# Macaron stack on one core: when the relative-distance rows of the first attention are read back from DRAM

## The chip, the cores and the metric

The kernel runs on one core of one Trainium2 chip (trn2). The metric is the device time of one execution in microseconds (us); where several executions were timed, the median is given.

## What is computed

The reference is a stack of four "macaron" layers in float32 over a stream x of 16 sequences of 256 tokens with 128 features. Each layer adds half a feed-forward block, an attention, and half a feed-forward block again, each on a layer-normalised copy of x. The four kinds are: product-key experts with an attention with relative distances (layer 0); windowed attention and a gated feed-forward block with a rotary attention (layer 1); routed experts with full attention (layer 2); an int8 gated block with a latent attention (layer 3).

Only the attention of layer 0 matters here. It has 16 heads of 8 features, and its scores are a product of queries and keys plus a term for the distance between two tokens, which is computed against all distances and then shifted row by row:

```python
def _rel_shift(x):
    B, H, Lq, Lr = x.shape
    xp = jnp.concatenate([jnp.zeros((B, H, Lq, 1), x.dtype), x], axis=-1)
    xp = xp.reshape(B, H, Lr + 1, Lq)
    return xp[:, :, 1:].reshape(B, H, Lq, Lr)[..., Lr - Lq:]
x = x + _L0_attn_ref(_layernorm(x, axis=-1), L0_attn_Wq, L0_attn_Wk, L0_attn_Wv, L0_attn_Wr, L0_attn_u_bias, L0_attn_v_bias)
```

## The kernel before, in words

The stream X stays in SBUF, transposed (features on partitions, 4096 tokens along the free side). The blocks run one after another, each in a `Phase` with its own tiles and semaphores, with a barrier at the end. Within a phase the program of every engine is written out by hand, and the engines meet at semaphores.

`strip_attention(..., "rel", ...)`, whose tiles are named `l0att_...`, is the attention of layer 0. A **pair** is two heads of one sequence: there are 8 pairs in a sequence and 128 in all. A **half** t (0 or 1) is 128 of the 256 queries. Every engine walks through steps j, and does parts of several pairs in each; step j stands at place g = j % 8 of its sequence. The steps of all engines are made by `steps`: the steps before the loop written out, then a loop (`Fori`) of 7 passes with 16 steps each, then the last steps written out.

The distances of pair j+3 are prepared in step j, three steps ahead of the scores that need them:

- TensorE, `distance_rows` (L613): both heads' distance terms of one half into the PSUM tile `XP`, of which there is one.
- ScalarE, `keep_rows` (L772): `XP` copied into `XS`, 128 partitions by 768 floats. `XS` has room for two pairs, two halves each, so the copy for pair j waits until the write of pair j-2, same half, has landed (`written`). It counts up `x_kept`.
- SyncE, `write` (L513): waits for `x_kept` and stores that half of `XS`, 384 KB, to the DRAM tensor `shifted_rows`, which holds eight pairs.
- SyncE, `read` (L521): waits until that write has landed (`written`) and until VectorE has done with the pair four before (`shifted`), and then loads the half again with rows that are two elements shorter than they were stored, 256 KB, into `BD`. This shifts row r by r places, as `_rel_shift` does. `BD` holds four pairs.
- VectorE, `shift` (L861): waits for the two halves (`landed`), adds `BD` to the scores in `SC` and takes the row's extreme, four times for a pair (two heads, two halves). Both halves of `BD` are needed for the first head.

In its own step j VectorE does `shift` of pair j, head 0, both halves; the copy of the transposed exponentials of pair j-1 (L869); some work once in a sequence; `shift` of head 1; the strips (L874); and a second copy L869. ScalarE's step is: `XS` half 0 of pair j+3, two exponentials of pair j (L793), the strips of pair j+5 (L783), `XS` half 1, two more exponentials. TensorE's step is: distance rows half 0 (L613), strips (L649), transposes (L637), distance rows half 1, every second step the values (L673), the third strip (L655), transposes, the scores of pair j+1 (L626), and `extras` at places 2, 3, 4, 6 and 7 of the sequence.

SyncE has one instruction stream. What it waits for in a `read` also holds back the `write` behind it:

```python
def step(b, j):
    write(b, j + 3, 0)
    read(b, j + 2, 1)
    write(b, j + 3, 1)
    read(b, j + 3, 0)
```

`held` is the wait of both, and adds a count to a semaphore that nobody waits for (`passed`).

Of the kernel before, what the change touches and what calls it, by code (L numbers as in the profile page):

```python
# [132 lines left out]
def load(eng, dst, src, sem):  # L133

    return eng.dma_start(dst, src, allow_slow_non_contiguous=True).then_inc(sem, 16)
# [273 lines left out]
def strip_attention(nc, tag, kind, R, XN, A, W, ident, shifted=None):  # L409
# [19 lines left out]
    with Phase(nc, tag) as ph:  # L429
# [38 lines left out]
        def until(eng, sem, value):  # L468

            if not isinstance(value, int) or value > 0:  # L470
                eng.wait_ge(sem, value)

        def exists(b, j):
            return not isinstance(b, int) or 0 <= 16 * b + j < PAIRS
# [4 lines left out]
        def steps(eng, step):  # L479
            for j in range(-6, BEGIN):  # L480
                step(0, j)
            with eng.Fori(0, NB // 2 - 1) as b:
                for j in range(BEGIN, BEGIN + 16):
                    step(b, j)
            for j in range(BEGIN, 16 + TAIL):
                step(NB // 2 - 1, j)

        with nc.Block() as block:
            @block.sync
            def _(sp):  # L490
                load(sp, wq[:, :], W["q"], sm["loaded"])
                load(sp, wk[:, :], W["k"], sm["loaded"])
                load(sp, wv[:, :], W["v"], sm["loaded"])
                if not rel:
                    load(sp, wqx[:, :], W["q_crossed"], sm["loaded"])
                    load(sp, wkx[:, :], W["k_crossed"], sm["loaded"])
                    load(sp, wo[:, :], W["o"], sm["loaded"])
                    load(sp, mask[:, :, :], A["causal"], sm["loaded"])
                    load(sp, rt[:, :, :], A["rope8"], sm["loaded"])
                    return  # L500
                load(sp, ub[:, :], W["u"], sm["loaded"])
                load(sp, vb[:, :], W["v_bias"], sm["loaded"])
                load(sp, wr[:, :], W["r"], sm["loaded"])
                load(sp, emb[:, :], A["rel_emb"], sm["loaded"])

                def held(sem, value):
                    until(sp, sem, value)
                    sp.sem_inc(sm["passed"], 1)

                def write(b, j, t):  # L510
                    if exists(b, j):
                        held(sm["x_kept"], 2 * (16 * b + j) + t + 1)
                        sp.dma_start(shifted[j % 8, t], XS[:, j % 2, t, :, :]).then_inc(written[j % 2][t], 16)  # L513

                def read(b, j, t):

                    if exists(b, j):
                        held(written[j % 2][t], 16 * (8 * b + j // 2 + 1))
                        held(sm["shifted"], 4 * (16 * b + j - 3))
                        rows = shifted[j % 8, t].rearrange("r c -> (r c)")[2 * P - 2:2 * P - 2 + 2 * P * (WIN - 1)]  # L520
                        sp.dma_start(BD[:, j % 4, t, :, :],  # L521
                                     rows.rearrange("(r c) -> r c", c=2 * WIN - 2)[:, 0:2 * L]).then_inc(landed[j % 4][t], 16)

                def step(b, j):
                    write(b, j + 3, 0)
                    read(b, j + 2, 1)
                    write(b, j + 3, 1)
                    read(b, j + 3, 0)

                steps(sp, step)  # L530
                for p in range(PAIRS - 4, PAIRS):
                    for t in range(2):
                        sp.wait_ge(written[p % 2][t], 16 * (p // 2 + 1))
                        sp.wait_ge(landed[p % 4][t], 16 * (p // 4 + 1))
# [2016 lines left out]
```

## Time and profile before

| | |
|---|---|
| median of 3 runs | 6541.68 us (6528.03 to 6549.58) |
| the profiled execution, its own time | 6533.99 us |
| its span, first to last instruction | 6532.2 us |
| attention of layer 0, pairs in flight | about 640 to 1277 us of the span |
| busy over the whole span | PE 78%, VectorE 67%, ScalarE 49%, GpSimd 31% |
| mean granted TensorE clock | 0.875 of full speed |
| DMA engines, mean busy share | over 8 tenths in the slices of this attention, near 0 elsewhere |

The page gives busy time per engine, a strip of 40 slices of the span, the DMA queues, the chain that ended last (here it holds nothing but the very end of the program), the costliest groups of instructions and the DMA issues with their median time from issue to landing. An idle time is put down to what released the engine. The phases run one behind another, so that what a stage saves or costs goes straight into the whole.

### The profile page before, as it was taken

The numbers are of one execution on the slowest core, as the hardware profiler recorded it, in microseconds if no ns is written. First come the engines' busy times: TensorE is split into PE (matmuls) and PEld (weight loads), VectorE is DVE, ScalarE is ACT, GpSimd is POOL, SyncE is SP. The second block draws the span as 40 slices with busy tenths as digits, with TensorE's granted clock in tenths as the row PEclk, the third lists the DMA queues.
The fourth block names the chain that finished last, engine by engine and source line by source line (L and its number), as shares of the span: only waits on it lengthen the run. The fifth ranks groups of instructions, "written<-read, shape, count | busy, mean of one in ns | idle before, by whom it ended". The sixth has DMA issues, their size and how long they took to land. (4 is left out here: it accounts for less than half of the span.)

```text
span 6532.2 us, 113135 instructions
## 1 busy us (share of the span) xinstructions
PE 5127.0 (78%) x33035; PEld 3575.9 (55%) x33132; DVE 4390.1 (67%) x10948; ACT 3190.2 (49%) x5879; POOL 2009.9 (31%) x1367
## 2 busy tenths in 40 slices
PE   6777888867769969969979979965768648596777
PEld 5665555456647737726647737724533435343664
DVE  6997677679967737738867747737645268363774
ACT  6776777677755535537755535541121420203223
POOL 6995111079954314302224324300020000200110
PEclk8999999889989989989989989975579755798888
DMA  1000888600000000000000000000110000100000
GB/s 29 0 0 21 262 267 271 213 15 0 0 11 0 0 14 0 0 9 1 1 11 0 0 14 0 0 8 10 26 26 1 0 14 7 46 0 14 0 0 17
DMA packets 162591, 213.91 MB, mean 33 GB/s; under 512 B 54804, under 2 KB 90984, under 8 KB 162408
## 3 DMA queue, kind: packets, MB, share of 16 engines
q1 hardware_dynamic: 160360, 207.73, 10.5%
q0 software_dynamic: 2048, 4.20, 0.3%
q8 instruction: 59, 0.97, 0.1%
q14 instruction: 124, 1.02, 0.1%
HBM read 104.91 MB, written 106.95 MB: 32 GB/s over the span
## 5 line engine op out<-in xcount | busy, mean ns | idle before, releaser
L1836 POOL TENSOR_TENSOR l0b_S<-l0b_sim 128x1024 f32<-128x1024 f32 x256 | 494.0, 1967 | 149.1 <-ACT l0b_sim L1899 129.3
L1836 POOL TENSOR_TENSOR l0a_S<-l0a_sim 128x1024 f32<-128x1024 f32 x256 | 494.2, 1968 | 81.0 <-ACT l0a_sim L1899 62.5
L1969 DVE SCALAR_TENSOR_TENSOR l0b_w<-l0b_S,l0b_best,l0b_SG 128x1024 f32<-128x1024 f32 x256 | 311.1, 1276 | 8.6 <-ACT l0b_SG L1916 4.1
L1969 DVE SCALAR_TENSOR_TENSOR l0a_w<-l0a_S,l0a_best,l0a_SG 128x1024 f32<-128x1024 f32 x256 | 311.3, 1276 | 8.1 <-ACT l0a_SG L1916 4.4
L1871 PE MATMUL l0a_WT<-ident,l0a_w 128*128 128x128 f32 x2048 | 266.3, 285 | 63.4 <-DVE l0a_w L1969 58.2
L1871 PE MATMUL l0b_WT<-ident,l0b_w 128*128 128x128 f32 x2048 | 265.0, 284 | 64.1 <-DVE l0b_w L1969 58.9
L1871 PEld LDWEIGHTS l0a_WT<-ident,l0a_w 128*128 128x128 f32 x2048 | 235.6, 146 | 108.8 <-DVE l0a_w L1969 108.7
L1871 PEld LDWEIGHTS l0b_WT<-ident,l0b_w 128*128 128x128 f32 x2048 | 234.2, 145 | 109.7 <-DVE l0b_w L1969 109.5
L1916 ACT ACTIVATE l0a_SG<-l0a_S 128x1024 f32<-128x1024 f32 x256 | 260.0, 1024 | 53.1 <-DVE l0a_w L1969 47.6
L1916 ACT ACTIVATE l0b_SG<-l0b_S 128x1024 f32<-128x1024 f32 x256 | 260.0, 1024 | 52.8 <-DVE l0b_w L1969 47.7
L861 DVE CUSTOM_DVE_ANT_0 l0att_S<-l0att_SC,l0att_BD 128x256 f32<-128x256 f32 x512 | 202.9, 420 | 114.4 <-DMA l0att_BD<-shifted_rows 86.5
L2283 ACT ACT_TABLE_LOAD x16 | 20.5, 1283 | 510.4 <-PE l2ae_IO L2266 255.6
L772 ACT ACTIVATE l0att_XS<-l0att_XP 128x768 f32<-128x768 f32 x256 | 223.8, 874 | 91.9 <-PE l0att_XP L613 79.7
L793 ACT ACTIVATE l0att_E<-l0att_S,l0att_least 128x256 f32<-128x256 f32 x512 | 236.8, 502 | 59.1 <-DVE l0att_least L861 57.7
L869 DVE COPY l0att_ET<-l0att_TU 128x512 f32<-128x512 f32 x256 | 176.1, 688 | 53.9 <-PE l0att_TU L637 52.1
L1049 POOL TENSOR_TENSOR l1b_att_qk<-l1b_att_qk,l1b_att_fine 128x1024 f32<-128x1024 f32 x64 | 121.7, 1901 | 256.1 <-DVE l1b_att_fine L1328 256.1
L1049 POOL TENSOR_TENSOR l1a_att_qk<-l1a_att_qk,l1a_att_fine 128x1024 f32<-128x1024 f32 x64 | 121.7, 1901 | 255.2 <-DVE l1a_att_fine L1328 255.2
L793 ACT ACTIVATE l1att_E<-l1att_S,l1att_least 128x128 f32<-128x128 f32 (+1 forms) x512 | 191.6, 446 | 15.0 <-DVE l1att_least L861 14.8
L1042 POOL TENSOR_TENSOR l1a_att_qk<-l1a_att_m 128x1024 f32<-128x1024 f32 x66 | 155.6, 2357 | 98.3 <-DVE l1a_att_m L1309 98.3
L1042 POOL TENSOR_TENSOR l1b_att_qk<-l1b_att_m 128x1024 f32<-128x1024 f32 x66 | 155.6, 2357 | 97.6 <-DVE l1b_att_m L1309 97.6
L2370 PE MATMUL l2bc_OUT<-l2bc_hot,l2bc_part 128*128 128x512 bf16 x752 | 167.9, 384 | 16.2 <-DVE l2bc_hot L2402 13.1
L2370 PE MATMUL l2ac_OUT<-l2ac_hot,l2ac_part 128*128 128x512 bf16 x752 | 167.7, 383 | 16.4 <-DVE l2ac_hot L2402 13.1
(707 smaller groups left out, 14300.9 us busy)
## 6 DMA issues: line engine op xcount, KB each, us to landing
shifted_rows<-l0att_XS SPq DMA_DIRECT2D x256, 384.0 KB, 4.2
l0att_BD<-shifted_rows SPq DMA_DIRECT2D x256, 256.0 KB, 3.7
enter_raw<-L_attn_w SPq DMA_DIRECT2D x4, 512.0 KB, 6.8
token_rows<-l2ar_rows SPq DMA_DIRECT2D x32, 64.0 KB, 1.5
l2ae_wgt<-L_ffn_gate_w SPq DMA_DIRECT2D x32, 64.0 KB, 2.0
l2ae_wut<-L_ffn_up_w SPq DMA_DIRECT2D x32, 64.0 KB, 2.0
l2ae_wdt<-L_ffn_down_w SPq DMA_DIRECT2D x32, 64.0 KB, 2.1
token_rows<-l2br_rows SPq DMA_DIRECT2D x32, 64.0 KB, 1.5
```

The lines of the kernel that those rows point to most:

```text
L772: act.activation(XS[:, j % 2, t, :, :].rearrange("p c h -> p h c"), XP[:, :, 0:WIN], ACT.Copy).then_inc(sm["x_kept"], 1)
L793: act.activation(E[:, j % 2, h, t, 0:keys(t)], S[:, j % 2, h, t, 0:keys(t)], ACT.Exp, bias=least[:, j % 2, h, t:t + 1], scale=-1.0).then_i ...
L861: dve.tensor_tensor_reduce(S[:, j % 2, h, t, 0:keys(t)], SC[:, h, t, 0:keys(t)], add, -scale, 3e38, ALU.add, ALU.min, least[:, j % 2, h, t ...
L869: dve.tensor_copy(ET[:, j // 2 % 2, 2 * (j % 2) + h, :, :], TU[:, h % NT, 0:len(blocks), :]).then_inc(sm["et_copied"], 1)
L1042: pool.tensor_tensor(qk[:, t, :, :, :], m1[:, :, :, :], m2[:, :, :, :], ALU.add).then_inc(sm["rotated"], 1)
L1049: pool.tensor_tensor(one, one, share, ALU.mult).then_inc(sm["qk_ready"], 1)
L1836: pool.tensor_tensor(S[:, h, :].rearrange("p (a c) -> p a c", a=NK), a, c, ALU.add).then_inc(sm["summed"], 1)
L1871: o = pe.matmul(WT[:, n // 4, (n % 4) * P:(n % 4 + 1) * P], w[:, h % W_RING, n * P:(n + 1) * P], ident[:, :], start=h == 0 and n % 4 == 0, ...
L1916: act.activation(SG[:, h % SG_RING, :], S[:, h, :], ACT.Sigmoid).then_inc(sm["sigm"], 1)
L1969: dve.scalar_tensor_tensor(w[:, h % W_RING, :], S[:, h, :], best[:, s, h, 7:8], SG[:, h % SG_RING, :], ALU.is_ge, ALU.mult).then_inc(sm["w ...
L2283: act.activation(xT[:, s, :], IO[:, s, 0:P], ACT.Copy).then_inc(sm["copied"], 1)
L2370: o = pe.matmul(OUT[:, :], part[:, k, n, :], hot[:, n % R, :], start=n == 0 and k == 0, stop=False)
```

## The change

The two reads in SyncE's step change places, and the read of half 0 is of pair j+2, where it was of pair j+3.

```diff
 def step(b, j):
     write(b, j + 3, 0)
+    read(b, j + 2, 0)
+    write(b, j + 3, 1)
     read(b, j + 2, 1)
-    write(b, j + 3, 1)
-    read(b, j + 3, 0)
```

Nothing else differs: the same 256 writes and 256 reads, the same tiles, the same semaphores and the same values that are waited for.

SyncE at the beginning of the stage, before. In these rows `written00` is pair parity 0, half 0, and so on; the semaphore of the writes is listed under a name that an earlier phase gave its number (`l0a_cands`), and is `x_kept` here.

```order
L513 DMA shifted_rows<-l0att_XS 128x768 [waits l0a_cands] x2
L521 DMA l0att_BD<-shifted_rows 128x512 [waits l0att_written00]
L513 DMA shifted_rows<-l0att_XS 128x768 [waits l0a_cands]
L521 DMA l0att_BD<-shifted_rows 128x512 [waits l0att_written01]
L513 DMA shifted_rows<-l0att_XS 128x768 [waits l0a_cands]
L521 DMA l0att_BD<-shifted_rows 128x512 [waits l0att_written10]
```

The same place with the change.

```order
L513 DMA shifted_rows<-l0att_XS 128x768 [waits l0a_cands] x3
L521 DMA l0att_BD<-shifted_rows 128x512 [waits l0att_written00]
L513 DMA shifted_rows<-l0att_XS 128x768 [waits l0a_cands]
L521 DMA l0att_BD<-shifted_rows 128x512 [waits l0att_written01]
L513 DMA shifted_rows<-l0att_XS 128x768 [waits l0a_cands]
L521 DMA l0att_BD<-shifted_rows 128x512 [waits l0att_written10]
```

Three writes stand before the first read, where two did: every read has moved behind one more write, and from there on reads and writes take turns as before. If the halves are numbered through, k = 1 to 256, the read of half k stood behind the write of half k+1 and now stands behind the write of half k+2.

SyncE at the end of the stage, before (`l0a_summed` is the number that `shifted` has here):

```order
L521 DMA l0att_BD<-shifted_rows 128x512 [waits l0att_written00,l0a_summed]
L513 DMA shifted_rows<-l0att_XS 128x768 [waits l0a_cands]
L521 DMA l0att_BD<-shifted_rows 128x512 [waits l0att_written01,l0a_summed]
L513 DMA shifted_rows<-l0att_XS 128x768 [waits l0a_cands]
L521 DMA l0att_BD<-shifted_rows 128x512 [waits l0att_written10,l0a_summed]
L521 DMA l0att_BD<-shifted_rows 128x512 [waits l0att_written11,l0a_summed]
```

The same place with the change.

```order
L521 DMA l0att_BD<-shifted_rows 128x512 [waits l0att_written00,l0a_summed]
L513 DMA shifted_rows<-l0att_XS 128x768 [waits l0a_cands]
L521 DMA l0att_BD<-shifted_rows 128x512 [waits l0att_written01,l0a_summed]
L521 DMA l0att_BD<-shifted_rows 128x512 [waits l0att_written10,l0a_summed]
L521 DMA l0att_BD<-shifted_rows 128x512 [waits l0att_written11,l0a_summed]
```

Three reads stand behind the last write, where two did. No other engine's instructions move.

## Rows read from the trace of the kernel before

**Rows 1.** Page, and engines from 640 to 1277 us: x, then busy, granted clock, DMA share, GB/s
```profile
shifted_rows<-l0att_XS SPq DMA_DIRECT2D x256, 384.0 KB, 4.2
l0att_BD<-shifted_rows SPq DMA_DIRECT2D x256, 256.0 KB, 3.7
...
core 0: us, PE busy (x) PEld busy (x) DVE busy (x) ACT busy (x) POOL busy (x), PEclk, DMA share, GB/s
640.00:1277.00 637.00, 516.80 (x4968) 329.92 (x4969) 452.14 (x1555) 485.84 (x911) 92.56 (x90) 0.95 0.85 264
```

**Rows 2.** Waits of SyncE's queue: us in total, times, longest
```profile
SPq L508 <- DMA shifted_rows<-l0att_XS: 342.6, 253, 3.6
...
SPq L508 <- ACT l0att_XS L772: 31.3, 14, 22.2
```

**Rows 3.** Timeline of SyncE's queue from 950 us: start, us
```profile
950.47 0.32 SPq L521 DMA_DIRECT2D l0att_BD<-shifted_rows  x1
951.09 0.32 SPq L513 DMA_DIRECT2D shifted_rows<-l0att_XS  x1
952.86 0.32 SPq L521 DMA_DIRECT2D l0att_BD<-shifted_rows  x1
953.39 0.32 SPq L513 DMA_DIRECT2D shifted_rows<-l0att_XS  x1
955.34 0.32 SPq L521 DMA_DIRECT2D l0att_BD<-shifted_rows  x1
955.85 0.32 SPq L513 DMA_DIRECT2D shifted_rows<-l0att_XS  x1
958.07 0.32 SPq L521 DMA_DIRECT2D l0att_BD<-shifted_rows  x1
...
960.41 0.32 SPq L521 DMA_DIRECT2D l0att_BD<-shifted_rows  x1
```

**Rows 4.** Instructions on XS from 630 to 951.0 us, and timeline of ScalarE
```profile
L772 ACT ACTIVATE l0att_XS<-l0att_XP x128: 842/872/920, 640.9 to 950.9; 128x768 f32<-128x768 f32 x128
L513 SPq DMA_DIRECT2D shifted_rows<-l0att_XS x125: 314/320/1947, 641.9 to 948.5; - x125
...
946.10 0.87 ACT L772 ACTIVATE l0att_XS<-l0att_XP 128x768 f32<-128x768 f32 x1
...
955.76 0.90 ACT L772 ACTIVATE l0att_XS<-l0att_XP 128x768 f32<-128x768 f32 x1
```

**Rows 5.** Instructions on BD, whole stage: who waited, and DMA from issue to landing
```profile
  DMA l0att_BD<-shifted_rows: 86.5, 79
  issue: 24.8, 15
...
DMA to landing us min/median/max: 2.6/3.7/6.2
```

**Rows 6.** Waits from 641 to 1280 us (total, times, longest), and landing of the writes
```profile
ACT l0att_XS L772 <- DMA shifted_rows<-l0att_XS: 8.9, 14, 2.4
...
DMA to landing us min/median/max: 2.3/4.2/6.7
```

**Rows 7.** XS copies of ScalarE in stretches of 16 halves and over 112 pairs: first and last start
```profile
L772 ACT ACTIVATE l0att_XS<-l0att_XP x17: 862/882/904, 777.2 to 812.2; 128x768 f32<-128x768 f32 x17
L772 ACT ACTIVATE l0att_XS<-l0att_XP x17: 842/877/906, 812.2 to 855.1; 128x768 f32<-128x768 f32 x17
L772 ACT ACTIVATE l0att_XS<-l0att_XP x17: 852/878/920, 855.1 to 890.4; 128x768 f32<-128x768 f32 x17
...
L772 ACT ACTIVATE l0att_XS<-l0att_XP x225: 842/873/920, 689.3 to 1241.1; 128x768 f32<-128x768 f32 x113
```

**Rows 8.** Timeline of VectorE at the end of a pass of the loop
```profile
771.30 0.42 DVE L861 CUSTOM_DVE_ANT_0 l0att_S<-l0att_SC,l0att_BD 128x256 f32<-128x256 f32 x1 [4.99 <-issue]
```

**Rows 9.** Timeline of ScalarE, a step in which it never waits
```profile
974.09 0.91 ACT L772 ACTIVATE l0att_XS<-l0att_XP 128x768 f32<-128x768 f32 x1
974.88 0.88 ACT L793 ACTIVATE l0att_E<-l0att_S,l0att_least 128x256 f32<-128x256 f32 x2
975.67 0.58 ACT L783 ACTIVATE l0att_strips<-l0att_PJ 128x512 bf16<-128x512 f32 x1
976.14 0.87 ACT L772 ACTIVATE l0att_XS<-l0att_XP 128x768 f32<-128x768 f32 x1
976.89 0.89 ACT L793 ACTIVATE l0att_E<-l0att_S,l0att_least 128x256 f32<-128x256 f32 x2
977.84 0.89 ACT L772 ACTIVATE l0att_XS<-l0att_XP 128x768 f32<-128x768 f32 x1
```

**Rows 10.** Timeline of VectorE, a shift that waits for its read, and the exponential behind it
```profile
954.40 0.42 DVE L861 CUSTOM_DVE_ANT_0 l0att_S<-l0att_SC,l0att_BD 128x256 f32<-128x256 f32 x1 [1.38 <-DMA l0att_BD<-shifted_rows]
...
954.87 0.51 ACT L793 ACTIVATE l0att_E<-l0att_S,l0att_least 128x256 f32<-128x256 f32 x1 [0.59 <-DVE l0att_least L861]
```

## The prediction

> **What bounds the stage now.** The change touches one stage, so I read the strip of slices first, then the waits of SyncE's own queue, then its timeline, and last what the engines behind it wait for. In the stage the DMA engines are busy 0.85 of the time, and every compute engine has idle time left: PE 516.8, ScalarE 485.8 and VectorE 452.1 of 637 us [rows 1]. SyncE stands 342.6 us in 253 waits for a write to land, 1.35 us each, and only 31.3 us in 14 waits for ScalarE's copies [rows 2]. It is hardly ever out of work: data is ready, and it is the queue that is late.
>
> The timeline shows the pattern [rows 3]: a read, then 0.5 to 0.6 us behind it a write, a pause, a read, a write. By the counts, 128 XS copies had begun at 951.0 us and 125 writes [rows 4], so the write at 951.09 is of half 126, whose copy began at 946.10 and ended at 946.97: it went out 4.1 us after it could have. The read of half 126 is the one at 955.34, that is 4.25 us after its write, the median landing of a write (4.2) [rows 1, 3]. And right behind it, at 955.85, goes the write of half 128. So there is a **loop in the queue**: write k, its landing (4.2), read k, write k+2 (0.53 behind it), which is one pair on. It allows a pair every 4.73 us. 128 pairs of it are 605 us, and with the 31.3 us in which SyncE did wait for ScalarE 637: all of the stage. Where the loop lags, both ends suffer: ScalarE waits 8.9 us for room in XS [rows 6], VectorE 86.5 us, in 79 waits, for reads to land [rows 5].
>
> **What the engines would do without it.** The XS copies give the pace. 17 copies span 8 pairs: 35.0 us from 777.2 to 812.2, then 42.9, then 35.3 again [rows 7]. The long one holds an end of a loop pass, at which VectorE stands 5.0 us for nothing the profile shows [rows 8]. After such a stop the queue has caught up, the next 8 pairs run at the engines' own pace, and then the lag is built up again. I take 35.0 us for 8 pairs (4.37 a pair) as the pace of the three compute engines together. Over the 112 pairs from 689.3 to 1241.1 us, 551.8 us now, that is 14 x 35.0 = 490, plus all 24.8 us of those stops [rows 5, 8] = 515. The most that can be won is 37 us there. On the 16 pairs outside it is between 0 (the first writes go out at once, and the last have none behind them) and 5 us, that share of the same. The whole term therefore lies between 0 (the next limit stands where this one did) and 42.
>
> **The change, part by part.** Instructions, bytes and waits stay; each read moves behind one more write. *Writes:* write k+3 now stands behind the wait for write k, issued three halves before. Three halves are 6.6 us even at 4.37 a pair, against a landing of 4.2: that wait costs nothing, and a write goes out as soon as its copy is done. The cover is 2.4 us wide; of today's landings only the longest, 6.7 us [rows 6], would outlast it. *Reads:* read k waits for write k+2, so for a copy one pair later. Half 128 was read at 960.41 [rows 3]. With the change its read follows the write of half 130, whose copy began at 955.76 and ended at 956.66 [rows 4]; the write goes 0.1 us after that and the read 0.53 later, at 957.3. The read moves back in the program and still goes out 3 us earlier, because the writes no longer lag. *What is late next:* the read of half 1. From the end of the XS copy behind which it goes to the shift that needs it lie two steps, less 2.92 us (the copy of half 1 ends that long after the step's first copy began) plus 0.70 (of the two exponentials' 0.88 us the second takes the last 0.5, so that it begins some 1.17 into its step, and its shift must start 0.47 ahead of it) [rows 9, 10]. Of this, 0.1 goes to issue the write, 0.53 until the read, 0.1 to wake VectorE. A landing may thus take two steps less 2.95 us. At 4.37 a pair this is 5.8 us; the step shown took 3.75 [rows 9], and with a neighbour at the mean pace it is 5.2. A read lands in 3.7 now [rows 5]. It will go right behind a write: the 4.2 of that write, less 0.53, plus its own 0.262 MB at 310 GB/s (264 GB/s at a share of 0.85 [rows 1]), an estimate of 4.5 us. It fits, narrowly in the short steps, and the longest landing of today (6.2) does not. *The tail:* three reads instead of two behind the last write, 0.3 us of issue each, beside other work.
>
> **DMA engines.** 0.85 x 637 / 128 = 4.23 us of all 16 engines for a pair [rows 1]. At 515/112 = 4.60 us a pair they would be busy 0.92. That is below the limit, though landings may grow as it is neared. The page "HBM Reference", section Specifications, of the Trainium skill has a core that streams alone at about 425 GB/s; a pair's 1.31 MB would then be 3.1 us, an estimate, and the engines never near their limit. By that page the sum would be the full 37. The trace speaks for less (264 GB/s at 0.85), and I go by the trace.
>
> **The sum.** 37 us, less some 3 us for reads that miss their shift in the short steps and at the higher load, and nothing taken for the ends: **34 us**. Against the profiled execution that is 6534.0 - 34 = 6500 us; that execution lies 7.7 us under the median of its three runs, so against the median it is 6541.7 - 34 = **6508 us**. A measurement of this kernel can tell about 0.3%, 20 us, from no change (the three runs span 21.6 us).
>
> **Rivals.**
> *A. The transfers are the bound already.* The share of 0.85 would then be about as full as the engines get in this mix, and the writes that go out earlier merely wait in the rings. For it: a landing takes 4.2 us under load. Against it: 8 pairs do run in 35.0 us [rows 7], 0.97 of the engines by 4.23 a pair. If the same 0.92 share costs 2 us more in every landing, half of the 37 us goes: about 15, 6525 us; at worst none.
> *B. Slower: the reads come too late.* Each read now stands behind 384 KB of the next write. The stage is as slow as today when the landing of read half 1 takes two steps of 4.93 (551.8/112) less 2.95 = 6.9 us; beyond it each us more stretches a pair by half a us. At 7.5 us it is 0.3 x 128 = 38 us slower, 6580 us. For it: 6.2 us occurs [rows 5]. Against it: the median is 3.7 and my estimate 4.5. The page "DMA: Bandwidth & Descriptors" of the Trainium skill says in "Two DMAs through the same engine are not ordered" that within a queue descriptors start in order, so a read does stand behind the write's; and its rules for kernel authors want a DMA issued early and waited for late, while this change puts reads later in the program. Taken by the letter that speaks for B; rows 3 and 4 show that in time the read is earlier.
> *C. More than that.* All waits for transfers go, 86.5 + 8.9 = 95.4 us [rows 5, 6], as if each lay on the path: 6446 us. Against it: most of VectorE's 79 waits only shift idle time that ScalarE or PE would have had, and 35.0 us for 8 pairs is a floor of the engines.
> *D. Nothing happens*, since the lag of the writes only fills slack: 6542. Against it: the long stretches of 8 pairs.
>
> **Chances.** My case 0.57; C, or something between it and mine, 0.08; A 0.20, of which 0.08 still gains more than 20 us and 0.12 does not; D 0.05; B 0.10. That gives faster 0.57 + 0.08 + 0.08 = 0.73, same 0.12 + 0.05 = 0.17, slower 0.10. The range: down to 42 us and 10 us of scatter, 6490; up to no gain and a few us of scatter, 6545. It leaves out B beyond that and C.
>
> **What would show it.** SyncE's waits for writes to land fall from 342.6 us below 100, and its waits for ScalarE grow to most of the rest. A write goes out 0.1 to 0.6 us after its copy. ScalarE's 8.9 us vanish, VectorE's 86.5 fall below 40. The DMA share rises to about 0.9, the 112 pairs take about 518 us, and the landing of a read is 4 to 5 us. I am wrong if the writes go out early and the 112 pairs still take over 540 us (A), or if VectorE's waits for BD grow (B).

## The result and the profile after

| | before | with the change |
|---|---|---|
| median | 6545.63 us, 4 runs (6528.03 to 6557.44) | 6486.81 us, 4 runs (6484.09 to 6495.79) |
| ratio | | 0.9914, 95% interval 0.9892 to 0.9935 |
| profiled execution, span | 6532.2 us | 6486.0 us |
| first to last shift (L861 on `l0att_S`) | 649.0 to 1276.1: 627.1 us | 650.1 to 1223.9: 573.8 us |

The change is faster by 0.86%, 58.8 us between the medians and 46.2 us between the two profiled spans. The forecast of 34 us had the sign and the main mechanism right and was too small; 6486.81 lies 3 us below the range. "The stage" is from here on the time from the first to the last shift, in the one profiled execution of each kernel: other stages are left out of it. It lost 53.3 us, and 7.1 us came back ahead of it and behind it, where no instruction differs.

SyncE's waits in its own queue, with the change:

```profile
SPq L508 <- ACT l0att_XS L772: 317.3, 254, 22.7
SPq L508 <- DMA shifted_rows<-l0att_XS: 4.5, 9, 1.3
```

Against [rows 2] the two have changed places. SyncE now stands for ScalarE's copies, 254 times; for writes to land it stands 4.5 us where it stood 342.6. The queue is ready before its work is. In either kernel one wait of some 22 us in the row on ScalarE is the one for the stage's first copy and lies ahead of the first write.

Instructions on XS from 630 to 951.0 us, with the change:

```profile
L772 ACT ACTIVATE l0att_XS<-l0att_XP x140: 844/876/911, 642.0 to 950.8; 128x768 f32<-128x768 f32 x140
L513 SPq DMA_DIRECT2D shifted_rows<-l0att_XS x139: 314/320/936, 643.0 to 949.8; - x139
```

and, cut out of the timeline, one copy and the queue behind it:

```profile
950.80 0.88 ACT L772 ACTIVATE l0att_XS<-l0att_XP 128x768 f32<-128x768 f32 x1
...
951.78 0.32 SPq L513 DMA_DIRECT2D shifted_rows<-l0att_XS  x1
...
952.29 0.32 SPq L521 DMA_DIRECT2D l0att_BD<-shifted_rows  x1
```

Before, 128 copies had begun and 125 writes gone out by then [rows 4], and a write lagged 4.1 us. Now it is 140 and 139, and the write goes 0.10 us after its copy ends (950.80 + 0.88 = 951.68). Each trigger is now a copy, with write and read 0.5 us apart; before, it was a landing, with read and write 0.5 us apart [rows 3].

Landing of the writes, from the instructions on XS:

```profile
DMA to landing us min/median/max: 2.3/3.2/5.0
```

and VectorE's idle time ahead of L861 with the landing of the reads, from the instructions on BD:

```profile
  issue: 24.4, 14
  DMA l0att_BD<-shifted_rows: 2.7, 3
...
DMA to landing us min/median/max: 2.6/3.4/5.6
```

Both landings are shorter, 3.2 and 3.4 against 4.2 and 3.7 [rows 1, 5, 6], though the same bytes are moved in less time. VectorE waits 2.7 us for reads where it waited 86.5; ScalarE's 8.9 us for room in XS are gone. The stops that the profile puts down to nothing are the same, 24.4 against 24.8.

XS copies with the change: two stretches of 8 pairs and the 112 pairs of [rows 7]; then all copies ahead of these, those of them from the 8th on, and the copies behind:

```profile
L772 ACT ACTIVATE l0att_XS<-l0att_XP x17: 867/875/903, 684.2 to 719.0; 128x768 f32<-128x768 f32 x17
L772 ACT ACTIVATE l0att_XS<-l0att_XP x17: 857/876/906, 719.0 to 758.4; 128x768 f32<-128x768 f32 x17
L772 ACT ACTIVATE l0att_XS<-l0att_XP x225: 845/874/911, 684.2 to 1196.3; 128x768 f32<-128x768 f32 x113
...
L772 ACT ACTIVATE l0att_XS<-l0att_XP x23: 844/877/890, 642.0 to 684.2; 128x768 f32<-128x768 f32 x23
L772 ACT ACTIVATE l0att_XS<-l0att_XP x16: 862/882/890, 653.8 to 684.2; 128x768 f32<-128x768 f32 x16
L772 ACT ACTIVATE l0att_XS<-l0att_XP x10: 851/878/887, 1196.3 to 1214.0; 128x768 f32<-128x768 f32 x10
```

and the last three of them in the kernel before:

```profile
L772 ACT ACTIVATE l0att_XS<-l0att_XP x23: 844/861/897, 640.9 to 689.3; 128x768 f32<-128x768 f32 x23
L772 ACT ACTIVATE l0att_XS<-l0att_XP x16: 849/868/897, 652.5 to 689.3; 128x768 f32<-128x768 f32 x16
L772 ACT ACTIVATE l0att_XS<-l0att_XP x10: 852/866/882, 1241.1 to 1261.9; 128x768 f32<-128x768 f32 x10
```

The reader is to see two things. The 112 pairs take 512.1 us, 39.7 less: 34.8 us for 8 pairs without a stop, and 39.4 for this eight with one (others with a stop took 37.8 to 40.2). And the ends, which I had counted at nothing, gave 13.6 us: 48.4 to 42.2 ahead, and behind, from the 247th copy to the last shift, 35.0 (1241.1 to 1276.1) to 27.6 (1196.3 to 1223.9). Ahead, the first 8 copies span 11.6 and 11.8 us, so that nothing was won there; all of it lies in the 16 copies from the 8th on, 36.8 to 30.4 us. Behind, 3.1 us lie in the copies (20.8 to 17.7) and 4.3 between the last copy and the last shift (14.2 to 9.9).

The engines over the stage, and over the first of the stretches of 8 pairs, to be read beside [rows 1]:

```profile
650.10:1223.90 573.80, 490.94 (x4901) 316.80 (x4905) 444.80 (x1548) 473.39 (x898) 92.20 (x89) 0.98 0.88 290
684.20:719.00 34.80, 30.96 (x316) 20.11 (x315) 28.14 (x98) 29.97 (x58) 6.18 (x6) 1.00 0.94 310
```

From first to last shift the kernel before has a DMA share of 0.86 at 266 GB/s; now it is 0.88 at 290, and 0.94 at 310 GB/s while 8 pairs run without a stop. The granted TensorE clock rose too, from 0.95 to 0.98 over the stage. Where 8 pairs run without a stop it is 1.00 in both kernels, and they take 35.0 us (777.2 to 812.2) and 34.8; so the clock is not what sets that pace. What it adds in the slower stretches was not separated from the waits.

### The profile page after: what moved, and what is told of

The parts are those of the page before. It is cut to its first block and busy times, and to the rows that moved or that the text cites. A ratio compares the mean times of both kernels' runs of the same rounds, so it can differ in the third digit from the quotient of the medians.

```text
span 6486.0 us, 113128 instructions
## 1 busy us (share of the span) xinstructions
PE 5117.7 (79%) x33035; PEld 3577.2 (55%) x33132; DVE 4383.5 (68%) x10948; ACT 3185.1 (49%) x5879; POOL 2010.0 (31%) x1367
## 5 line engine op out<-in xcount | busy, mean ns | idle before, releaser
L861 DVE CUSTOM_DVE_ANT_0 l0att_S<-l0att_SC,l0att_BD 128x256 f32<-128x256 f32 x512 | 196.5, 418 | 29.5 <-issue 24.4
```

The lines of the kernel that those rows point to most:

```text
L861: dve.tensor_tensor_reduce(S[:, j % 2, h, t, 0:keys(t)], SC[:, h, t, 0:keys(t)], add, -scale, 3e38, ALU.add, ALU.min, least[:, j % 2, h, t ...
```

## The experiments

Theory (**queue loop**): write k, its landing, read k, write k+2 form a loop through SyncE's one stream, and a pair cannot be faster than landing + 0.53 us. (By the issue times in the trace of before, a median of 4.33 us from a write to its read and of 0.53 from there to the next write but one: 4.86 us a pair, 622 us for 128, of the 627.1 of the stage.) Rivals: the start decides whether writes lag; room in XS; the transfers themselves.

| run | order or edit | median us (95% interval of the ratio) | stage us | writes land | reads land | SyncE waits for writes |
|---|---|---|---|---|---|---|
| before | | 6545.63 | 627.1 | 4.2 | 3.7 | 342.6 |
| the change | | 6486.81 (0.9892 to 0.9935) | 573.8 | 3.2 | 3.4 | 4.5 |
| loop_only | new order in the loop | 6502.12 (0.993 to 0.9966) | 583.8 | 3.2 | 3.4 | 49.4 |
| ends_only | new order at the ends | 6525.97 (0.9966 to 0.9987) | 609.1 | 4.2 | 3.8 | 301.6 |
| half0 | new order for half 0 | 6488.64 (0.9908 to 0.9941) | 574.5 | 3.7 | 3.4 | 180.1 |
| xs4 | XS twice as deep, old order | 6538.05 (0.9988 to 1.0009) | 628.9 | 4.2 | 3.8 | 352.9 |
| older_rows | other rows read, old order | 6540.25 (0.9986 to 1.0008) | 625.8 | 4.2 | 3.8 | 348.4 |
| reads_k3 | reads one half later | 6513.40 (0.9933 to 0.9967) | 595.4 | 3.1 | 3.3 | 1.5 |
| reads_k4 | reads two halves later | 6687.24 (1.0183 to 1.0262) | 773.1 | 2.5 | 2.9 | 0.2 |
| extra_load | the change and a second read | 6552.52 (1.0006 to 1.003) | 638.9 | 5.8 | 5.2 | 137.6 |
| read_first | read ahead of write k+2 | 6537.90 (0.9986 to 1.0007) | 632.2 | 4.3 | 3.8 | 304.1 |
| read_first_late | the same, reads one half later | 6518.22 (0.9938 to 0.9971) | 612.4 | 4.5 | 4.0 | 3.7 |
| unrolled_old | loop written out, old order | 6551.34 (1.0011 to 1.0033) | 643.2 | 4.4 | 3.9 | 384.5 |
| unrolled | loop written out, new order | 6471.65 (0.9877 to 0.991) | 554.8 | 3.4 | 3.7 | 9.4 |

The medians stand beside different runs of the kernel before (6537.07 to 6545.63 us), so that the ratio is what compares two rows. The stage is read from one execution each. The 112 pairs, with the old order inside the loop, took 551.8 us in before, 545.0 in ends_only, 551.4 in xs4 and 548.7 in older_rows: a difference of a few us in the stage says nothing.

**Where the gain lies: loop_only and ends_only.** Both have `old` and `new` as steps and change over at the loop's two ends, with every half read once. Of ends_only:

```diff
-                steps(sp, step)
...
+                for j in range(-6, BEGIN):
+                    new(0, j)
+                read(0, BEGIN + 2, 0)
+                with sp.Fori(0, NB // 2 - 1) as b:
+                    for j in range(BEGIN, BEGIN + 16):
+                        old(b, j)
...
```

> The new order in the 112 steps of the loop, the old one in the steps written out before and behind it. I time the stage from the first to the last shift (L861 on l0att_S): 627.1 us before, 573.8 with the change, 53.3 less, of which 39.7 lie between the 17th and the 241st XS copy, 6.2 ahead and 7.4 behind. Queue loop (my theory: a write stands behind a read that waits for an earlier write): the gain belongs to the steps whose order is new, so about 40 us, the stage 587 (583 to 591). Rival, the lag is a state that the start decides (once the first writes lag, the whole stage does): the stage stays over 610.

> The reverse: new order in the steps before and behind the loop, old order inside it. Queue loop: the two ends give 6.2 + 7.4 = 13.6 us, the stage 613.5 (609 to 618); with the run of the loop alone the two gains add up to 53. Rival, the start decides: the stage is near 574.

(The window meant in the first of them lies between the 23rd and the 247th copy, not the 17th and the 241st; its numbers are right.) Measured were 583.8 and 609.1 us, 43.3 and 18.0 less than before. The gain follows the steps whose order is new, so the start does not decide: in loop_only the 112 pairs took 507.6 us, 44.2 less, and the ends nothing less; in ends_only the ends gave 11.1 us, and the 112 pairs 6.8, with their order unchanged. The two add up to 61.3 us where both together gave 53.3. The 8 us between are of the size by which single executions differ, and stay open. The times of whole executions fell by 36.7 and 12.9 us between the medians.

**One of the two loops cut: half0.** Against the kernel before:

```diff
                 def step(b, j):
                     write(b, j + 3, 0)
-                    read(b, j + 2, 1)
-                    write(b, j + 3, 1)
-                    read(b, j + 3, 0)
+                    read(b, j + 2, 0)
+                    read(b, j + 2, 1)
+                    write(b, j + 3, 1)
```

> Old order for half 1, new for half 0: write half 0, read half 0 (behind write k+2), read half 1 (behind write k+1), write half 1. Instructions and bytes as before. Queue loop: one of the two loops is cut, the other (write of half 1, its landing, its read, next write of half 1) stays and allows a pair every landing + 0.53 us. If landings stay at 4.2, that is 4.73 and the stage stays at 620 to 627. If they fall to the 3.2 of the changed kernel, it is 3.7, nothing binds and the stage is near 574; writes of half 1 would still go out behind a wait. Rival, the transfers themselves (each write directly behind a read is what makes landings long): landing between 3.2 and 4.2, about 3.7, stage about 600.

574.5 us, all of the gain, though SyncE still stands 180.1 us for writes to land. The rival that a write directly behind a read is what makes landings long had the landing right, 3.7, and with it wanted about 600 us; as an account of the time it falls. At 3.7 the loop that is left allows a pair every 4.23 us; by the issue times of half 1 in the trace (3.90 from a write to its read, 0.51 to the next write) it is 4.41, as long as the 4.37 that the engines take. It is not there to be seen in the time although it is there in the waits: a loop costs only what it is longer than the next one.

**Room in XS: xs4.**

```diff
-            XS = ph.sb("XS", [P, 2, 2, WIN, 2])
+            XS = ph.sb("XS", [P, 4, 2, WIN, 2])
...
-        written = [[ph.sem(f"written{i}{t}") for t in range(2)] for i in range(2)] if rel else None
+        written = [[ph.sem(f"written{i}{t}") for t in range(2)] for i in range(4)] if rel else None
```

> The order of before, and XS with room for four pairs, with a written semaphore for each. Queue loop: ScalarE's 8.9 us of waits for room go, but SyncE's loop of 4.73 us a pair stays, so that the stage shortens by 0 to 9 us (618 to 627), waits of SyncE for writes to land stay over 300 us and VectorE's waits for BD stay or grow. Rival, room in XS (the writes lag because the copies cannot run ahead): the stage falls by over 25 us, below 600.

628.9 us, 1.9 over what I expected and within what single executions differ by, and a ratio of 0.9998. ScalarE's wait for room is gone, and nothing was won: VectorE's for reads is 95.0, where it was 86.5 in before and 100.4 in older_rows, whose XS is as before. More buffer ahead of a queue that is late only makes the line longer.

**Bytes that have just landed: older_rows.**

```diff
-                        rows = shifted[j % 8, t].rearrange("r c -> (r c)")[2 * P - 2:2 * P - 2 + 2 * P * (WIN - 1)]
+                        src = j if isinstance(b, int) and 16 * b + j == 0 else j - 1
+                        rows = shifted[src % 8, t].rearrange("r c -> (r c)")[2 * P - 2:2 * P - 2 + 2 * P * (WIN - 1)]
```

> The order and all waits of before, but each read loads the rows of the pair before (the first pair its own), so the distance term is that of another pair. The bytes that a read loads then landed a pair earlier instead of just now. Theory 1, reading bytes that have only just landed makes transfers slow: the landing of reads falls from 3.7 towards 3.2 and that of writes from 4.2 towards 3.7, and the loop of before gives landing + 0.53 = about 4.3 us a pair, which no longer binds: stage 580 to 595. Theory 2, it is the order of write and read in the rings: landings stay 4.2 and 3.7, the stage 620 to 628.

Landings 4.2 and 3.8, stage 625.8: which rows are read makes no difference, and theory 1 falls.

**Later still: reads_k3 and reads_k4.** The second of them, against the kernel before:

```diff
                 def step(b, j):
                     write(b, j + 3, 0)
-                    read(b, j + 2, 1)
+                    read(b, j + 1, 0)
                     write(b, j + 3, 1)
-                    read(b, j + 3, 0)
+                    read(b, j + 1, 1)
```

> Every read one more half later than in the change: behind write k+3. Budget of the read of half 1 by my sum, now counted from the end of the copy of half 0 one step ahead of the shift: one step - 0.87 + 0.70 - 0.73 = one step less 0.90 us. At a landing of 3.4 (changed kernel) steps of 4.3 or more still fit; the steps of 3.75 miss by 0.55 each, two of them in eight steps, 1.1 x 16 = 18 us: stage 574 + 18 = 592 (580 to 600). If reads profit further from being later (a theory in which distance from the write is what makes a read fast), landing falls below 3.4 and the stage stays at 574 to 580.

> Every read two halves later than in the change: behind write k+4. This is the rival in which reads come too late, forced. Budget of the read of half 1: one step less 2.95 us, so that a step must last 2.95 + 3.4 = 6.35 us: stage about 128 x 6.35 = 813 us (760 to 850), the whole about 6725. SyncE waits for nothing but ScalarE, and VectorE waits about 1.9 us for BD in nearly every step. If the stage stays below 650, my budget is wrong and the reads had more room than I counted.

595.4 us for a forecast of 592. The budget "one step less 0.90 us" had two late reads in eight steps, some 32 in all; VectorE waited 99 times for reads, 69.1 us in total. So the reads come late as the budget says, but in far more steps, and that the number is within 4 us is in part luck. At k+4 the stage took 773.1 us, in the range and below the 813. VectorE's idle time ahead of L861 there, and the landing of its reads:

```profile
  DMA l0att_BD<-shifted_rows: 264.4, 136
...
DMA to landing us min/median/max: 2.5/2.9/4.7
```

The budget used a landing of 3.4, and with fewer bytes in a second a read landed in 2.9: 2.95 + 2.9 = 5.85 us a pair, 749 us, nearer to what was measured. So the rival in which reads come too late is real. It stands one half away for a part of the gain (21.6 us of stage) and two halves away for a loss of 146 us against the kernel before.

**How full the DMA engines were: extra_load.** Every read of the changed kernel is followed by a second one:

```diff
+            spare = ph.sb("spare", [P, 4, 2, L, 2])
...
+                        held(spared[j % 4][t], 16 * (4 * b + j // 4))
+                        sp.dma_start(spare[:, j % 4, t, :, :],
+                                     rows.rearrange("(r c) -> r c", c=2 * WIN - 2)[:, 0:2 * L]).then_inc(spared[j % 4][t], 16)
```

> The change, plus a second read of the same rows into a spare tile behind every read: 1.84 MB a pair instead of 1.31, and 512 DMAs of reading instead of 256. It adds 0.4 to 0.5 us of issue to SyncE each. If the DMA share of 0.85 is work that bytes cost (310 GB/s at most), a pair needs 1.84/310 = 5.9 us and the stage is about 128 x 5.9 = 760. If it is partly latency and the engines can do 425 GB/s, as the page HBM Reference (section Specifications) of the Trainium skill has it for a core that streams alone, a pair needs 4.3 us, and the stage stays near 574, at most 600.

The engines from 640 to 1290 us:

```profile
640.00:1290.00 650.00, 522.52 (x4957) 332.77 (x4957) 448.31 (x1539) 485.44 (x906) 93.00 (x91) 0.94 0.97 361
```

The stage took 638.9 us, and both forecasts fail: 361 GB/s went through, where the share of 0.85 had made me expect 310 at most. In SyncE's queue around 955 us:

```profile
951.60 0.53 SPq L515 DMA_DIRECT2D shifted_rows<-l0att_XS  x1
...
957.66 0.32 SPq L523 DMA_DIRECT2D l0att_BD<-shifted_rows  x1
...
958.74 0.32 SPq L515 DMA_DIRECT2D shifted_rows<-l0att_XS  x1
```

These are a write, its own read and the third write behind it: 7.14 us for three halves, or 4.76 a pair, 609 us for 128. With landings of 5.8 us the loop through the third write binds too, and SyncE stands 137.6 us in 202 waits for writes. So this run gives 361 GB/s as a rate that the engines can move in this mix, with their share at 0.97, and not a limit that is shown; the 425 GB/s of the Trainium skill (HBM Reference, section Specifications) was not reached, and no run here shows whether it could be. At 361 GB/s the 1.31 MB of a pair need 3.6 us, less than the 4.37 of the engines: transfers alone were not the bound.

**Order in the rings: read_first and read_first_late.** "Rings" stands in the expectations for the queue's list of transfers. At each copy the read is issued first; in the second kernel it is the read of one half earlier.

```diff
                 def step(b, j):
-                    write(b, j + 3, 0)
-                    read(b, j + 2, 0)
-                    write(b, j + 3, 1)
-                    read(b, j + 2, 1)
+                    copied(b, j + 3, 0)
+                    read(b, j + 1, 1)
+                    write(b, j + 3, 0)
+                    copied(b, j + 3, 1)
+                    read(b, j + 2, 0)
+                    write(b, j + 3, 1)
```

> The change, but at every copy the read goes first and the write 0.53 us behind it: SyncE waits for the copy, issues read k, then write k+2. Both are issued at the same moments as in the change, in the other order, which is the order in the rings that the kernel before had. If order in the rings makes the landings (a read that starts first keeps the engines waiting for its data, and holds up the write), the read lands in about 3.4 to 3.7 and the write in about 4.2; if the better landings of the change (3.2 and 3.4) come from the later read alone, they stay at 3.2 to 3.4. In both cases no queue loop binds and the stage stays at 574 to 585: a long landing costs nothing when nothing waits behind it. If the long landing as such was what cost time before, the stage goes back above 600.

> The run read_first kept the queue loop, since write k+2 stood behind the wait of read k in it; this one has the same pattern at every copy (wait for the copy, a read, 0.5 us later the write), but with the read of one half earlier, so that write k+3 is the first behind the wait for write k. Reads go at the moments of reads_k3, 0.5 us sooner, so that this is the run to compare: there the write goes first, landings 3.1 (write) and 3.3 (read), stage 595.4. Order in the rings as the cause of the long landings: write about 4.2, read 3.4 to 3.8, and the stage all the same 585 to 605, since nothing waits behind the landing. Lateness of the read (or the loop's own rhythm) as the cause: landings stay at about 3.1 to 3.4 and the stage is 580 to 600. A stage above 620 would mean that read-before-write costs time without any queue loop, and my account of the change would fall.

read_first was planned wrongly. Its write k+2 stands behind the wait of read k for write k, which is the queue loop, and its expectation said that there was none. It took 632.2 us with 304.1 us of waits, at a ratio of 0.9996: the order of before in other words, and by its time once more that order's cost. The last sentence of its expectation would take a stage above 600 for the price of the long landings themselves; with the loop in it, the run cannot show that.

read_first_late has no such loop, 3.7 us of waits. SyncE's queue in it:

```profile
955.14 0.32 SPq L521 DMA_DIRECT2D l0att_BD<-shifted_rows  x1
955.57 0.37 SPq L513 DMA_DIRECT2D shifted_rows<-l0att_XS  x1
```

Beside reads_k3, in which the write goes first and the rest is the same, writes land in 4.5 instead of 3.1 us and reads in 4.0 instead of 3.3. The kernel before has the same order, a read and 0.5 us behind it a write, and its landings of 4.2 and 3.7 go with it. The stage took 612.4 us, over the 585 to 605 that I gave it and 17.0 more than reads_k3: VectorE waits 73.9 us for reads, against 69.1, and ScalarE 57.7 us for VectorE's results where it waited 46.6. That the longer landing costs this time is not shown. Whole executions do not bear it out: the ratios are 0.9955 (0.9938 to 0.9971) and 0.995 (0.9933 to 0.9967), 27.0 and 28.8 us between the medians, and the profiled execution of read_first_late is the slowest of its four, 9 us over their median. It did not bring back the time of before. Why a read ahead of a write lengthens both landings isn't settled.

**The loop written out: unrolled_old and unrolled.**

```diff
-            with eng.Fori(0, NB // 2 - 1) as b:
-                for j in range(BEGIN, BEGIN + 16):
-                    step(b, j)
+            if rel:
+                for b in range(NB // 2 - 1):
+                    for j in range(BEGIN, BEGIN + 16):
+                        step(b, j)
...
```

> The order of before, with the 7 passes of the loop written out, so that no engine jumps back (the page's 24.8 us of stops of VectorE at L861 go as far as they belong to the jumps). Queue loop: a pair cannot be faster than landing 4.2 + 0.53 = 4.73 us, the stops only gave the queue time to catch up, so that the stage stays at 615 to 627, at most 12 us shorter. Rival, stops and queue add up: the stage loses over 18 us, below 609.

> The change, with the 7 passes of the loop written out. No queue loop binds here, the engines' own pace does: 35.0 us (measured 34.8) for 8 pairs throughout, so that the stops' 24.4 us are gained in full or nearly: stage 550 to 556, the whole about 6465. If the stops come from code that has to be loaded, and more code makes more of them, the stage stays near 574.

XS copies between 719 and 1020 us, in the old order and then in the new one:

```profile
L777 ACT ACTIVATE l0att_XS<-l0att_XP x120: 843/872/922, 719.3 to 1019.9; 128x768 f32<-128x768 f32 x120
```

```profile
L777 ACT ACTIVATE l0att_XS<-l0att_XP x136: 857/880/917, 720.9 to 1017.7; 128x768 f32<-128x768 f32 x136
```

A pair takes 300.6/59.5 = 5.05 us in the old order and 296.8/67.5 = 4.40 in the new. VectorE's stops at L861 are gone in both (0.6 and 0.4 us). In the new order that is worth 19.0 us of stage, within the forecast. In the old order the stage got 16.1 us longer, 643.2 (ratio 1.0022, 1.0011 to 1.0033), which is beyond my 615 to 627. The pauses had been free, since the queue's loop ran on in them. The rest is the loop itself, which got longer: the writes land in 4.4 us, and by the issue times a pair takes a median of 4.55 + 0.43 = 4.98 us, 637 us for 128, where it took 4.86. Why landings are longer without pauses was not tested. With the pauses gone, the order of the reads alone is worth 643.2 - 554.8 = 88.4 us of stage, 79.7 between the medians: more than in the kernel as it stands.

unrolled, at 6471.65 us and a ratio of 0.9894 (0.9877 to 0.991), is the fastest of all. It is the change with this one edit, and its program is longer.

## Why the prediction was right and wrong

- *"There is a loop in the queue": right, though its sum closed by luck.* I added 605 us of loops and the 31.3 us in which SyncE waited for ScalarE to 637. But 22.2 of these 31.3 are the one wait ahead of the first write [rows 2], so that no more than 9 lie in the stage. What fills it is a longer loop: 4.73 left out the 0.1 to 0.2 us between a landing and the read, and by the issue times it is 4.86 us, 622 of the 627.1. Waits for landing went from 342.6 to 4.5 us, the lag of a write from 4.1 to 0.1 us. Doubling the buffer, reading other rows and starting the stage otherwise did not take the loop away; the order alone did, wherever it was applied.
- *"The most that can be won is 37 us there", over the 112 pairs: right as a size, 39.7, and 2.7 too low for a bound.* The pace of the three engines is 34.8 us for 8 pairs rather than 35.0, which is 2.8 us in 14 such stretches, and the stops stayed at 24.4.
- *"Nothing taken for the ends": wrong, and the term that took the result out of the range.* It measured 13.6 us. My reason, that the first writes go out at once, held for the first 8 copies alone (11.6 and 11.8 us). From the 8th to the 23rd, with the exponentials running, before took 36.8 us, 4.91 a pair, which is the queue loop's 4.86; with the change they took 30.4, 4.05 a pair, quicker than the 4.37 of the middle. A loop of fixed length costs most where the work around it is least. Why the engines are quicker there was not tested; the granted clock over the copies ahead was 0.93 before and 1.00 now, and its part is not separated. At the other end I wrote that the last writes have nothing behind them. But they lagged too: by the issue times the last one went out 4.7 us after its copy had ended, and now 0.1, and its read and the last shifts waited for it. That is the 4.3 us between the last copy and the last shift.
- *"Less some 3 us for reads that miss their shift": wrong.* VectorE waits 2.7 us in all. The landing of a read behind a write was estimated at 4.5 and is 3.4. The estimate took its 310 GB/s from the DMA share, which extra_load (361 GB/s) shows to be too low as a limit, and left the landing of the write at 4.2, where it became 3.2 with the write going first.
- *"At 4.60 us a pair they would be busy 0.92": too high, 0.88 over the stage.* In the quick stretches it was 0.94, and the landings got shorter all the same. Rival A rested on this share. extra_load moved 361 GB/s where the changed kernel moved 290. I let the trace's share speak against the rate of the Trainium skill (HBM Reference, section Specifications). By its 425 GB/s transfers would be no bound, and they were none; the rate itself was reached in no run.
- *Rival B (reads too late): right in its mechanism, not its place.* It begins one half further on (reads_k3, 21.6 us of the 53.3 lost) and turns the sign at two. The budget forecast the first within 4 us, with a third of the late reads that there were, and the second within 40.
- *Rival C (all 95.4 us of waits): wrong for this kernel*, which has 53.3. *Rival D: wrong*; the lag did not only fill slack.
- *The base.* 34 us would have been 39.7 + 13.6 = 53.3 with the measured terms: of the 19.3 us missing, 13.6 are the ends, 3 the reads that missed nothing, and 2.7 the pace. 6541.68 - 53 = 6489 is the median to within 2 us. The profiled executions show 46.2, since 7.1 us more went elsewhere; four runs of before span 29 us, so that the 58.8 between the medians is no sharper than its interval.

## What to carry to other kernels

When a queue waits for a landing and something that is ready stands behind that wait, follow it round until it meets itself: landing plus issue is then a period, and it holds however deep the buffers are. Put the wait so far back that it is always over when it is reached, then count how much later the consumer gets its data: here this loss began one half further on. Cost such a loop in every stretch by the pace that the engines would have there, the quick stretches at the start and the end first, and take neither a DMA share nor a wait's total for the time that can be won: 180 us of waits cost nothing in half0. Look for the same kind of loop in every experiment too: it stood in read_first and in extra_load, whose expectations reckoned with none.

## What the runs showed of the hardware

- Two transfers issued 0.5 us apart on one queue land differently by their order: write of 384 KB first, 3.1 us and 3.3 for the read of 256 KB; read first, 4.5 and 4.0 (reads_k3 and read_first_late). Whether the bytes read have just landed makes no difference (older_rows).
- A DMA share of 0.86 over the stage went with 266 GB/s, 0.88 with 290, and in extra_load, from 640 to 1290 us, 0.97 with 361 GB/s. It is not proportional to bytes, and the 310 GB/s that the prediction worked out of it as a limit were passed.
- The stops at the end of a loop's pass (24.8 us at L861, up to 5.0 each) disappear when the passes are written out. What the engines do in them was not tried.
